# Receptance projection of a fused RWKV block as seven half-width products, in the steady loop of a one-core Trainium2 kernel

## What is computed

```python
x_prev = pad(x[:, :-1, :], ((0, 0), (1, 0), (0, 0)))      # x is layernorm(x)
xk = x * time_mix_k + x_prev * (1.0 - time_mix_k)          # xv, xr alike
k = einsum('btd,ed->bte', xk, W_k)
v = einsum('btd,ed->bte', xv, W_v)
r = sigmoid(einsum('btd,ed->bte', xr, W_r))                # the receptance
wkv = _wkv_scan(k, v, time_decay, time_first)
x = x + einsum('btd,ed->bte', r * wkv, W_o)
h = silu(tlin(x, w1, s1)) * tlin(x, w2, s2)                # x is layernorm(x)
h = gelu(tlin(h, h1, sh1)); h = gelu(tlin(h, h2, sh2))     # 1024 to 1024 each
x = x + tlin(h, w3, s3)
```

## Time and profile before

| | |
|---|---|
| median of three runs | 1486.68 us (1486.51 to 1488.37) |
| profiled execution, its own time | 1485.31 us |
| its span, first to last instruction | 1483.6 us |
| mean granted TensorE clock | 1.000 |
| busy, share of the span | PE 99%, DVE 81%, ACT 73%, POOL 14% |

### The profile page before, as it was taken

The page is one execution under the profiler, slowest core; times in us unless marked ns, Lnnn a source line. Parts: engine busy times, 40 slices in busy tenths (PEclk is TensorE's granted clock), DMA queues, the critical chain, the costliest instruction groups (busy, mean ns, idle before and its releaser), DMA issues.

```text
span 1483.6 us, 28137 instructions
## 1 busy us (share of the span) xinstructions
PE 1473.6 (99%) x10326; PEld 1324.7 (89%) x10326; DVE 1205.3 (81%) x1554; ACT 1077.1 (73%) x1626; POOL 204.3 (14%) x173
## 2 busy tenths in 40 slices
PE   8999999999999999999999999999999999999999
PEld 6989898998989989899898989989899898998998
DVE  7797887868888687887878878788886878878655
ACT  6895776867768777686867868677587776868655
POOL 1314020110201102011030210202011020110200
PEclk9999999999999999999999999999999999999999
DMA  9977474755737467374674746657475673746654
GB/s 352 380 264 270 148 231 118 222 160 171 242 97 242 125 204 227 106 248 117 203 210 130 235 130 205 176 168 227 103 240 139 193 234 97 250 117 201 192 178 140
DMA packets 94926, 285.28 MB, mean 192 GB/s; under 512 B 9136, under 2 KB 33328, under 8 KB 92976
## 3 DMA queue, kind: packets, MB, share of 16 engines
q1 hardware_dynamic: 86736, 277.01, 57.5%
q0 software_dynamic: 8160, 7.87, 4.5%
HBM read 250.76 MB, written 33.03 MB: 191 GB/s over the span
## 4 chain that ended last, share of the span: by engine, by line
PE 93%; DVE 3%; ACT 2%; issue 1%; POOL 1%; DMA 0%; DVEq 0%; POOLq 0%; ACTq 0%
PE acc L645 27%; PE acc L647 26%; PE att L554 10%; PE acc L619 7%; PE acc L620 7%; PE acc L671 4%; PE acc L673 4%; PE att L577 3%; PE att L533 2%; PE att L620 1%; PE att L619 1%; DVE stage L1724 1%; DVE op_lo L1595 0%; PE acc L773 0%; PE acc L771 0%
## 5 line engine op out<-in xcount | busy, mean ns | idle before, releaser
L645 PE MATMUL acc<-op_hi,ring 128*128 128x256 f32 x3360 | 810.7, 286 | 0.5 <-issue 0.5
L647 PE MATMUL acc<-op_lo,ring 128*128 128x256 f32 x3360 | 788.8, 279 | 0.0
L645 PEld LDWEIGHTS acc<-op_hi,ring 128*128 128x128 f32 x3360 | 632.2, 188 | 18.6 <-issue 17.6
L647 PEld LDWEIGHTS acc<-op_lo,ring 128*128 128x128 f32 x3360 | 632.0, 188 | 11.1 <-issue 10.0
L1595 DVE TENSOR_TENSOR op_lo<-blocks,op_hi 128x1024 fp32r<-128x1024 f32 (+2 forms) x271 | 338.9, 1265 | 98.3 <-ACT op_hi L1007 90.9
L1007 ACT ACTIVATE op_hi<-blocks 128x1024 fp32r<-128x1024 f32 (+2 forms) x263 | 283.7, 1091 | 82.8 <-DVE blocks L1590 74.9
L619 PE MATMUL acc<-x_hi,w_rnd 128*128 128x512 f32 x420 | 167.6, 399 | 0.0
L620 PE MATMUL acc<-x_lo,w_rnd 128*128 128x512 f32 x420 | 165.9, 395 | 0.0
L2018 POOL TENSOR_TENSOR v_sb<-mix_v,v_sb 128x1024 f32<-128x1024 f32 (+1 forms) x19 | 39.4, 2072 | 833.7 <-DVE r_sb L1522 824.8
L1047 ACT ACTIVATE blocks<-acc,vec 128x256 f32<-128x256 f32 x268 | 104.9, 475 | 60.9 <-PE acc L647 60.8
L1047 ACT ACTIVATE blocks<-parts,vec 128x256 f32<-128x256 f32 x240 | 102.3, 497 | 56.2 <-DVE parts L1652 47.9
(11 more groups left out here) (185 smaller groups left out, 2116.8 us busy)
## 6 DMA issues: line engine op xcount, KB each, us to landing
ring<-scratch SPq DMA_DIRECT2D x427, 512.0 KB, 4.2
scratch<-stage SPq DMA_DIRECT2D x11, 1024.0 KB, 12.4
stage<-in_w_ffn SPq DMA_DIRECT2D x10, 1024.0 KB, 10.9
x_in<-in_x SPq DMA_DIRECT2D x32, 256.0 KB, 4.8
out<-x_next SPq DMA_DIRECT2D x30, 256.0 KB, 5.1
out<-mix_v POOLq DMA_DIRECT2D x30, 256.0 KB, 4.4
scratch<-in_w_ffn SPq DMA_DIRECT2D x4, 1024.0 KB, 15.0
ring<-stage SPq DMA_DIRECT2D x7, 512.0 KB, 9.4
```

The costliest lines, as they stand in the source:

```text
L645: pe.matmul(out, act(w), act(op_hi[:, k, c, :]), start=(begins and c == 0 and m % 2 == 0), stop=False, skip_group_check=True)
L647: mm = pe.matmul(out, act(w), act(op_lo[:, k, c, :]), start=False, stop=(c == QC - 1), skip_group_check=True)
```

## The change

In the 14 rounds of the loop the two calls of `project` for r (j = 4, 5) are replaced by a seven-product scheme on 2 by 2 blocks. The weights are cut into four blocks of 128 by 128, `wr11` to `wr22`, and the inputs `mix_r` into four of 128 channels by 256 columns, `r11` to `r22` (chunk, sequence). POOL makes the four sums of weight blocks `wr_s1` to `wr_s4` once, before the loop (`r_weights`). DVE makes four sums of inputs per tile, `r_t1` to `r_t4` (`r_difference`), kept in `x1_next`. PE does the seven products of 256 columns at four places (`r_point`, k = 0 to 3: two, two, two and one product). In between, ACT copies partial results (`r_copy`) and takes exponentials in pieces (`r_exp`), and DVE adds the last two quarters (`r_sum`). `gain` stands behind `t1b` now, the last value copy is waited for there too, and `exp(WHOLE, i + 1, 3)` stands ahead of `hiT23`. Projections of k and v stay where they were. The core of the diff:

```diff
+            def r_matmul(out, w, x, start, stop):
+                return pe.matmul(out, w, x, start=start, stop=stop, skip_group_check=True)
+            def r_point(t, k):
+                u = t - 2
+                if k == 0:
+                    pe.wait_ge(WHOLE.dve_mix.sem, WHOLE.dve_mix.at(t))
+                    pe.wait_ge(WHOLE.act_kvr.sem, WHOLE.act_kvr.at(t, 2 * DC))
+                    pe.wait_ge(dve_tr.sem, dve_tr.at(u, 1))
+                    r_matmul(R_Z, wr_s1, r_t1, True, False)
+                    pe_r.add(r_matmul(R_Y, wr11, r11, False, False))
+                if k == 1:
+                    pe.wait_ge(act_r.sem, act_r.at(u, 2))
+                    pe.wait_ge(dve_tr.sem, dve_tr.at(u, 3))
+                    WHOLE.pe_kvr.add(r_matmul(R_X, wr_s2, r_t2, False, False))
+                    mm = r_matmul(R_Y, wr12, r21, False, True)
+                    pe_r.add(mm)
+                if k == 2:
+                    pe.wait_ge(act_r.sem, act_r.at(u, 3))
+                    pe.wait_ge(WHOLE.act_kvr.sem, WHOLE.act_kvr.at(t, 2 * DC + 1))
+                    WHOLE.pe_kvr.add(r_matmul(R_X, wr_s3, r_t3, False, False))
+                    pe_r.add(r_matmul(R_Z, wr_s4, r22, False, True))
+                if k == 3:
+                    pe.wait_ge(dve_r.sem, dve_r.at(u, 1))
+                    pe.wait_ge(dve_tr.sem, dve_tr.at(u, 4))
+                    pe_r.add(r_matmul(R_X, wr22, r_t4, False, True))
...
                     step(i, 0, 5)
-                    project(WHOLE, i + 1, [4])
-                    step(i, 0, 6)
+                    step(i, 0, 6, [0])
+                    r_point(i + 1, 0)
+                    step(i, 0, 6, [1])
                     step(i, 1, 0, [0])
-                    project(WHOLE, i + 1, [5])
+                    r_point(i + 1, 1)
                     step(i, 1, 0, [1])
+                    r_point(i + 1, 2)
                     step(i, 1, 1)
+                    r_point(i + 1, 3)
                     step(i, 1, 2)
...
+            def r_copy(t, k):
+                act.wait_ge(pe_r.sem, pe_r.at(t - 2, (1, 1, 2)[k]))
+                dst, src = ((R_X, R_Y), (r_p5, R_Z), (r_u2, R_X))[k]
+                act_r.add(act.activation(dst, src, ACT.Copy))
+            def r_exp(t, k):
+                if k == 0:
+                    act.wait_ge(pe_r.sem, pe_r.at(t - 2, 2))
+                    WHOLE.act_kvr.add(act.activation(r_out[0][0], R_Y, ACT.Exp, scale=-1.0))
+                if k == 1:
+                    act.wait_ge(pe_r.sem, pe_r.at(t - 2, 4))
+                    WHOLE.act_kvr.add(act.activation(r_out[1][0], R_X, ACT.Exp, scale=-1.0))
+                if k == 2:
+                    act.wait_ge(dve_r.sem, dve_r.at(t - 2))
+                    late_half = by_seq(r_sb[:])[:, :, 1, :]
+                    WHOLE.act_exp.add(act.activation(late_half, late_half, ACT.Exp, scale=-1.0))
...
                 hiT1(i)
-                copy_kvr(WHOLE, i + 1, [4])
+                r_copy(i + 1, 0)
+                r_copy(i + 1, 1)
                 g21(i, 0)
+                exp(WHOLE, i + 1, 3)
+                r_copy(i + 1, 2)
+                r_exp(i + 1, 0)
                 hiT23(i)
-                exp(WHOLE, i + 1, 3)
                 p1(i, 1)
                 hiB21(i)
-                copy_kvr(WHOLE, i + 1, [5])
-                exp_r(WHOLE, i + 1)
+                r_exp(i + 1, 1)
+                r_exp(i + 1, 2)
                 p5(i, 1)
...
+            def r_difference(t, k):
...
+                dst, a, b = ((r_t1, r12, r11), (r_t3, r22, r12), (r_t2, r22, r_t1), (r_t4, r21, r_t2))[k]
+                dve_tr.add(dve.tensor_tensor(dst, a, b, ALU.subtract))
+            def r_sum(t, k):
+                dve.wait_ge(pe_r.sem, pe_r.at(t - 2, 3))
+                dst, a, b = ((r_out[1][1], R_X, r_p5), (r_out[0][1], R_Z, r_u2))[k]
+                dve_r.add(dve.tensor_tensor(dst, a, b, ALU.add))
...
                 loB11(i)
+                r_difference(t, 0)
+                r_difference(t, 1)
                 c12(i, 0)
-                gain(WHOLE, t)
+                r_difference(t, 2)
+                r_difference(t, 3)
                 c22(i, 0)
                 t1b(i)
+                gain(WHOLE, t)
                 recurrence(WHOLE, t, 0)
                 t23b(i)
                 loT1(i)
                 recurrence(WHOLE, t, 1)
                 loB22(i)
+                r_sum(t, 0)
+                r_sum(t, 1)
                 loT23(i)
...
+            r_weights(0, wr_s1, wr21, wr22, False)
+            r_weights(1, wr_s2, wr_s1, wr11, True)
+            r_weights(2, wr_s3, wr11, wr21, True)
+            r_weights(3, wr_s4, wr12, wr_s2, True)
             tile_deviation(1, 1)
```

More of the change, by code:

```diff
@@ L177, in build @@
         wm = sb("wm", [P, 4, DC, D])
+        wr_sums = sb("wr_sums", [P, 4, P])
         x_in = sb("x_in", [P, NB, D])
@@ L254, in build @@
         LAST_BLOCK = BANK[6][:, 0:D]
+        wr11, wr12, wr21, wr22 = (wm[:, 2, c, e * P:(e + 1) * P] for e in range(2) for c in range(2))
+        wr_s1, wr_s2, wr_s3, wr_s4 = (wr_sums[:, k, :] for k in range(4))
+        r11, r12, r21, r22 = (mix_r[:, c, n * SEG:(n + 1) * SEG] for c in range(2) for n in range(2))
+        r_t1, r_t2, r_t3, r_t4 = (x1_next[:, k, :] for k in range(4))
+        r_p5, r_u2 = r_t1, r_t2
+        R_X, R_Z, R_Y = BANK[6][:, 0:SEG], BANK[7][:, 0:SEG], BANK[7][:, SEG:2 * SEG]
+        r_out = [[r_sb[:, e, n * SEG:(n + 1) * SEG] for n in range(2)] for e in range(2)]
         PAIR_OF, ALL = (slice(0, 2), slice(2, 4)), slice(0, QC)
@@ L347, in build @@
         ld_ring = [tally(f"ld_ring{k}", USES, 16) for k in range(SLOTS)]
+        pe_r, act_r, dve_r, dve_tr = (tally(n, k, ahead=0) for n, k in (("pe_r", 4), ("act_r", 3), ("dve_r", 2), ("dve_tr", 4)))
+        sum_r = ctx.enter_context(nc.semaphore("sum_r"))
         ld_x = tally("ld_x", n_seq, 16)
@@ L828, in mlp @@
                 pe.sem_inc(pe_half.sem, HALF_STEPS - PLAIN_STEPS)
+                pe.wait_ge(sum_r, 4)
                 with pe.Fori(1, NT - 1) as i:
@@ L836, in mlp @@
                     project(WHOLE, i + 1, [0, 1, 2])
-                    step(i, 0, 2, [0])
-                    step(i, 0, 2, [1])
+                    step(i, 0, 2)
                     project(WHOLE, i + 1, [3])
@@ L965, in exp_r @@
                 s.act_exp.add(act.activation(r_sb[:, :, s.cols], r_sb[:, :, s.cols], ACT.Exp, scale=-1.0))
+            def r_copy(t, k):
[13 more added lines that the diff above has]
+                    WHOLE.act_exp.add(act.activation(late_half, late_half, ACT.Exp, scale=-1.0))
             def seed_x(s, t):
+                if s is WHOLE and not isinstance(t, int):
+                    act.wait_ge(dve_r.sem, dve_r.at(t - 2))
                 act.wait_ge(s.act_kvr.sem, s.act_kvr.at(t))
@@ L1441, in first_running_max @@
                 link(s, dve.tensor_copy(carry_p[:, :, s.seqs], seq[:, :, s.seqs, SEG:SEG + 1]))
+            def r_difference(t, k):
+                if k == 0:
+                    dve.wait_ge(WHOLE.dve_mix.sem, WHOLE.dve_mix.at(t))
+                    dve.wait_ge(st_x1.sem, st_x1.at(t - 1))
+                if k == 2:
+                    dve.wait_ge(dve_tr.sem, dve_tr.at(t - 2, 1))
+                if k == 3:
+                    dve.wait_ge(dve_tr.sem, dve_tr.at(t - 2, 3))
+                dst, a, b = ((r_t1, r12, r11), (r_t3, r22, r12), (r_t2, r22, r_t1), (r_t4, r21, r_t2))[k]
[4 more added lines that the diff above has]
+                dve_r.add(dve.tensor_tensor(dst, a, b, ALU.add))
             def now_exponents(s, t):
@@ L1493, in gain @@
                 dve.wait_ge(s.act_exp.sem, s.act_exp.at(t, 2))
+                if s is WHOLE:
+                    dve.wait_ge(s.act_kvr.sem, s.act_kvr.at(t, 2 * DC))
                 if s is FIRST[0]:
@@ L1520, in gated_denominator @@
                 dve.wait_ge(s.act_exp.sem, s.act_exp.at(t))
+                if s is WHOLE:
+                    dve.wait_ge(s.act_kvr.sem, s.act_kvr.at(t))
                 settle(s, t)
@@ L2067, in _, with r_weights @@
             pool.sem_inc(WHOLE.pool_chain.sem, WHOLE.pool_chain.per)
+            def r_weights(k, dst, a, b, subtract):
+                if k:
+                    pool.wait_ge(sum_r, k)
+                pool.tensor_tensor(dst, a, b, ALU.subtract if subtract else ALU.add).then_inc(sum_r, 1)
+            r_weights(0, wr_s1, wr21, wr22, False)
+            r_weights(1, wr_s2, wr_s1, wr11, True)
+            r_weights(2, wr_s3, wr11, wr21, True)
+            r_weights(3, wr_s4, wr12, wr_s2, True)
             tile_deviation(1, 1)
```

## The result

The changed kernel takes 1509.36 us (median of 4 runs, 1507.7 to 1509.64), against 1487.36 us of the kernel before on the same chip (4 runs, 1486.51 to 1488.37): a ratio of 1.0151, with a 95% interval from 1.0138 to 1.0164. It is slower by 22 us, which is 1.57 us for each of the 14 rounds. I had forecast slower, by 0.78 us a round; 1509.36 lies above my range, which ended at 1505.

A forecast was written before the change was run, and what follows sets the result against it. PE was taken to bound the kernel, busy 99% at full clock. A 1.20 us wait less 0.42 us saved gave 0.78 us a round, 10.9 us over 14 rounds: 1497.6 us forecast, range 1493 to 1505.

The forecast's parts named there:

- a sign of being wrong: Listed signs: point 2's row missing or under 0.8 us, a wait for another engine, or `step(1, 2)` or `project_out` waiting for DVE.
- What bounds the kernel: In the 14 rounds time is the sum of PE's instructions; saved products and added waits count in full.
- What PE saves: Two r projections, 3.44 us, become seven half-width products, 3.02 us: 0.42 us saved a round.
- From 727.13 on, PE goes: half-step to 729.01: PE's schedule from the old first r projection's start: step 6's first half runs at once, point 2 is reached at 736.37.
- ACT's string: ACT's chain of copies, gelu, table load and exponentials ahead of point 2, tied to PE through `c22`, done at 737.41.
- My list of covers: Slack expected to hide other delays: 0.9 us before `step(1, 2)` (for `loT23`), 1.6 us before `project_out`.
- The wait of 1.20 us at point 2: PE waits at point 2 for ACT's third copy and first r exponential, from 736.37 to 737.57, each round.
- The sum: Wait less saving: 0.78 us a round, 10.9 us over 14 rounds.
- The table load: Ahead of ACT's first r exponential: 1.28 us for the load, the exponential 1.29 after its start.
- Rival 4: ACT drains 1.4 us before a load directly behind gelus: wait 2.6 us, time 1517 us; chance 1%.
- Rival 3: A second wait per round, before `step(1, 2)` or `project_out`, half to one microsecond: 1505 to 1512 us; chance 12%.
- Point 0, point 1 and POOL: No PE wait at the first two points (point 1's copies 0.7 us early); POOL's four weight sums, 2.9 us, hidden.

The follow-up runs named there:

- experiment 5: Kernel of experiment 4 with DVE's three sums for r placed behind `loT23` instead of behind the recurrence's first half: 1480.18 us, ratio 0.9951 to the kernel before.
- experiment 2: Changed kernel with point 0 ahead of step 6 of the first hidden layer, which is no longer split: 1497.61 us, ratio 1.0076.
- experiment 4: Changed kernel with its seven products laid out earlier, around steps 5 and 6, raw copies, three DVE sums and one exponential over r: 1484.93 us, ratio 0.9989.
- experiment 1: Kernel before, with only the first r projection moved behind the first half of step 6: 1509.78 us, ratio 1.0149.
- 3: Changed kernel plus four dead float32 instructions of 512 columns (1.72 us) ahead of step 6: 1510.34 us, ratio 1.0162.
- experiment 6: Changed kernel with ACT's exponential of the keys' mix moved behind the second r copy and first r exponential: 1512.4 us, ratio 1.0165.

## Where the prediction was right and where it was wrong

Slower was right, but not for the reason given: the wait that I had forecast for ACT, 1.20 us, measured 0.24, and the loss is a wait for another engine at another step, which I had named as a sign of being wrong.

- **What bounds the kernel**: right. PE bound before and after, at full clock, and each wait put on it came through in full: 1.63 us a round in the trace times 14 is 22.8, measured 22.0.
- **What PE saves**, 0.42 us a round: right. The half-width instructions took 0.217 each, no charge for going in and out of float32, and experiment 5 brings the 6 us home.
- **"From 727.13 on, PE goes: half-step to 729.01"**, in the part on when PE comes to each point: this is the step that failed. At 727.13 step 6 isn't free to start. It needs `c22`, which runs until 728.55 in the row that I quoted, and the r projection of 1.72 us that the change takes away from there had hidden it. I had used `c22` as the anchor of ACT's string and counted the projection only as work of PE; that it was also the cover of a wait I did not see. It had covered it with only 0.15 us to spare: 728.85 against 728.55 and a restart of 0.15. My list of covers had two entries, and the one that fell was not on it. It was worth 1.65 us a round, 23 us in all, which is the whole loss and a little more.
- **The wait of 1.20 us at point 2**: the string of ACT was right within 0.12 us where it runs freely (experiment 2), and the wait was 0.24, because PE comes late by the missed wait. It did not shrink to nothing, since ACT's gelus then wait for the end of step 6 and the same string runs from there to point 2.
- **The sum**, 1.20 - 0.42 = 0.78: measured 1.65 + 0.27 - 0.43, and 0.14 besides, most of it in slower short instructions behind point 3.
- **The table load**: 1.28 us, and 1.30 from its start to the exponential's, directly behind gelus. Rival 4 and the rule of the Trainium skill ("ScalarE: Activation LUTs", "What ACT_TABLE_LOAD costs", about 2.66 us a switch) are both refuted for this place.
- **Rival 3, a second wait per round**: its sum lay in the right region (1505 to 1512 us), by another wait and another place. The two covers that it names held in the changed kernel: no row of PE's waits has either of them. One of them, `loT23`, did fail in experiment 4, by 0.22 us a round, and gave back what it took in experiment 5. The cover of 1.6 us ahead of project_out never failed.
- **Point 0, point 1 and POOL**: no waits, as forecast. The four sums of weights took 0.46 us each, 57.0 to 59.1, in idle time of POOL.
- **What stays open**: why the short instructions between point 3 and `project_out` are slower by some 0.1 us a round. The fifth experiment is 6.7 us faster by the medians where its rounds give 6.3 and the products alone 5.9, a difference within the spread of the runs.

## What to carry to other kernels

When work is moved away from a place on the bounding engine, look at what it stood in front of: for the instruction that now comes first there, list all that it waits for and when each was ready in the trace, even where the old profile shows no wait at all. A wait that is hidden has no row among the waits; it shows only as another engine's instruction that ends while the moved work runs. And put filler of the same length in its place, or move the work alone: one such run (experiment 1 or 3) prices a cover by itself.

## What the runs showed that I had not expected

- A table load is placed at the first function of the new set, behind whatever precedes it in ACT's order. Ahead of a copy that would have waited the load was hidden (745.25 in the changed kernel; in experiment 6 that copy waits 1.16 us), behind it the load cost its 1.28 us in the string (748.55 in experiment 6). Which instruction of a set comes first decides whether the load is hidden.
- PE's restart behind a wait was 0.15 us after DVE's end (738.64 to 738.79) and cost some 0.07 more on the next instruction, where I had read 0.06 behind an ACT copy.
- A longer first wait on the bounding engine need not take the second one away: from experiment 2 to the changed kernel the first grew by 0.94 us (0.71 to 1.65), and the second shrank by only 0.11 (0.35 to 0.24). In the changed kernel ACT's gelus wait 0.67 us for PE in between, so ACT is late too.
